# Attention and feed-forward layer on one core: the output projection as three float32r passes, half of it inside the last head pair

## What is computed

```python
xn = _layernorm(x, axis=-1)
qkv = einsum('bsh,oh->bso', xn, w_qkv)                  # 16 heads of width 32
scores = where(causal, einsum('bhqd,bhkd->bhqk', q, k) * scale, min)
attn = einsum('bhqk,bhkd->bhqd', softmax(scores), v)
a = einsum('bsh,oh->bso', attn, w_o)                    # the output projection
gate, up = xn @ Wg.T, xn @ Wu.T                         # 4096 wide, weights are 4-bit codes times scales
out = x + a + (gelu(gate) * up) @ Wd.T
```

## Time and profile before

| | us |
|---|---|
| median of 3 runs | 1840.53 (1839.3 to 1840.86) |
| the profiled execution | 1840.19 |
| its span | 1838.4 |
| TensorE busy in the span | 1796.9 |
| VectorE, GpSimd, ScalarE busy | 1127.0, 721.6, 702.3 |

### The profile page before, as it was taken

The page is one execution under the profiler, slowest core; times in us unless marked ns, Lnnn a source line. Parts: engine busy times, 40 slices in busy tenths (PEclk is TensorE's granted clock), DMA queues, the critical chain, the costliest instruction groups (busy, mean ns, idle before and its releaser), DMA issues.

```text
span 1838.4 us, 28874 instructions
## 1 busy us (share of the span) xinstructions
PE 1796.9 (98%) x10496; PEld 1348.4 (73%) x10496; DVE 1127.0 (61%) x1724; ACT 702.3 (38%) x1151; POOL 721.6 (39%) x720
## 2 busy tenths in 40 slices
PE   7989999999999998999999999999999999999998
PEld 6877666666666654478888888888888888888887
DVE  5416666666666666457665675666566567566654
ACT  3323666666666664023232332232232323323322
POOL 1431778778778774021222222222222222222221
PEclk9999999999999998999999999999999999999999
DMA  8675043143143100521101101100110110110002
GB/s 286 218 215 151 10 102 73 37 102 73 37 102 72 38 17 21 197 69 35 35 0 34 34 0 34 34 26 9 34 34 0 34 34 3 31 34 0 1 1 92
DMA packets 73105, 108.59 MB, mean 59 GB/s; under 512 B 24704, under 2 KB 44784, under 8 KB 69360
## 3 DMA queue, kind: packets, MB, share of 16 engines
q1 hardware_dynamic: 73008, 107.34, 21.2%
HBM read 74.04 MB, written 29.59 MB: 56 GB/s over the span
## 4 chain that ended last, share of the span: by engine, by line
PE 60%; DVE 0%; issue 0%
PE p_up L51 6%; PE p_gate L51 6%; PE p_gate L49 6%; PE p_up L49 6%; PE p_gate L50 6%; PE p_up L50 6%; PE p_out L51 6%; PE p_out L49 6%; PE p_out L50 6%; PE p_out L1358 1%; PE p_gate L1358 1%; PE p_up L1358 1%; DVE acc L1288 0%
## 5 line engine op out<-in xcount | busy, mean ns | idle before, releaser
L1200 POOL TENSOR_SCALAR poly<-poly 128x1024 f32<-128x1024 f32 (+1 forms) x65 | 71.4, 1098 | 841.3 <-ACT poly L1162 841.3
L635 POOL TENSOR_TENSOR e_sum<-e_sb 128x512 f32<-128x512 f32 (+1 forms) x244 | 291.2, 1220 | 99.2 <-PE p_o L923 89.8
L771 DVE TENSOR_REDUCE max_part<-p_s 128x1 f32<-128x512 f32 x384 | 241.2, 683 | 51.5 <-PE p_s L855 50.2
L708 ACT ACTIVATE e_sb<-p_v 128x512 f32<-128x512 f32 (+3 forms) x427 | 216.5, 552 | 129.7 <-PE p_v L883 70.2
L1263 DVE SCALAR_TENSOR_TENSOR inter<-inter,gate 128x1024 f32<-128x1024 f32 (+1 forms) x65 | 78.6, 1209 | 248.4 <-ACT inter L1168 247.6
L855 PE MATMUL p_s<-k_stack,q_stack 96*128 96x512 f32 (+3 forms) x640 | 217.2, 393 | 0.7 <-DVE max_part L771 0.5
L767 DVE CUSTOM_DVE_ANT_0 recip<-p_s,score_mask 128x128 bf16<-128x128 f32 (+3 forms) x256 | 119.7, 486 | 156.0 <-PE p_s L855 153.9
L1161 ACT ACTIVATE gate<-p_gate 128x1024 f32<-128x1024 f32 (+1 forms) x65 | 66.0, 1015 | 354.6 <-PE p_gate L51 354.6
L49 PE MATMUL p_gate<-xn_hi,w_hi 128*128 128x512 f32 x512 | 199.6, 390 | 0.0
L50 PE MATMUL p_gate<-xn_lo,w_hi 128*128 128x512 f32 x512 | 199.2, 389 | 0.0
L51 PE MATMUL p_gate<-xn_hi,w_lo 128*128 128x512 f32 x512 | 199.2, 389 | 0.0
(11 more groups left out here) (146 smaller groups left out, 3090.6 us busy)
## 6 DMA issues: line engine op xcount, KB each, us to landing
q_stack<-qk_scratch SPq DMA_DIRECT2D x48, 256.0 KB, 6.5
k_stack<-qk_scratch SPq DMA_DIRECT2D x48, 256.0 KB, 7.2
qk_scratch<-out_hi SPq DMA_DIRECT2D x32, 256.0 KB, 2.6
qk_scratch<-out_lo SPq DMA_DIRECT2D x32, 256.0 KB, 3.3
scales<-in_gate_up_s SPq DMA_DIRECT2D x128, 64.0 KB, 2.3
xn_lo_scratch<-xn_lo SPq DMA_DIRECT2D x4, 1024.0 KB, 5.2
v_scratch<-o_sb SPq DMA_DIRECT2D x16, 256.0 KB, 2.6
xn_lo<-xn_lo_scratch SPq DMA_DIRECT2D x1, 4096.0 KB, 16.7
```

Of the source, the lines that this page charges most:

```text
L635: nc.gpsimd.tensor_tensor(*operands(k, i), ALU.add).then_inc(pool_summed, 1)
L708: nc.scalar.activation(e_sb[:, x % E_BUFS, 0:w], bank_st(x)[:, 0:w], ACT.Exp, scale=SCALE).then_inc(exp_done, 1)
L771: nc.vector.reduce_max(part, p_s[:, slot[n] % S_BUFS, 0:w], AX.X).then_inc(maxed, 1)
```

## The change

The projection is split like the other products: `w_o` into `wo_hi` and `wo_lo`, attention's output into a high part (copied by ScalarE) and a low part (subtracted by GpSimd), with three float32r matmuls for each product (`project_high`, `project_low`). A tile is one of four channel groups for one block of 512 tokens: 12 matmuls over four banks.

- The eight tiles of tokens 0 to 1023 are done in attention's block, in the four banks of `p_s`: four tiles in groups 75 to 78, between the transposed scores, and four behind group 79. The high and low parts have two slots each in a `k_stack` that is free by then. The weights are split in groups 70 to 74, into the `q_stack` of the even pairs. VectorE adds x for tokens 0 to 511 before the last division.
- The eight tiles of tokens 1024 to 2047 open the next block, with six slots in the second half of the weights' buffers.
- The first chunk of packed weights, and x for tokens 0 to 1023, are loaded in attention's block, into `rsum_rows`, `v_stack0`, `wo_sb` and a `k_stack`. In the next block x and `xn_lo` come in parts.
- At the front the values have six slots (four in `rsum_rows`, two in `o_sb`), the heads of pair 0 are loaded in halves, and units stand behind the tiles 5 to 14, five behind each: 50 instead of 44.

The core of the diff, with empty lines taken out:

```diff
+def project_high(nc, banks, g, wo_hi, wo_lo, a_hi, ots):
+    for ot in ots:
+        o = slice(ot * P, (ot + 1) * P)
+        nc.tensor.matmul(banks[ot], wo_hi[:, g, o], a_hi, start=g == 0, stop=False)
+        nc.tensor.matmul(banks[ot], wo_lo[:, g, o], a_hi, start=False, stop=False)
+def project_low(nc, banks, g, wo_hi, a_lo, ots):
+    for ot in ots:
+        last = nc.tensor.matmul(banks[ot], wo_hi[:, g, ot * P:(ot + 1) * P], a_lo, start=False, stop=g == KT - 1)
+    return last
...
+    V_SLOTS = 6
+    FIRST_COLS = S // 2
...
-    BEHIND_V = {v: 4 if v == 6 else 5 for v in range(6, TT - 1)}
+    BEHIND_V = {v: 5 for v in range(5, TT - 1)}
...
+        q_stack = [[stack_hi, stack_lo], [sb(f"q_stack1{a}", [P, S], F32R) for a in range(2)]]
+        k_stack = [[sb("k_stack00", [P, S], F32R)], [sb(f"k_stack1{a}", [P, S], F32R) for a in range(2)]]
+        xt_at = nc.sbuf_base
+        k_stack[0].append(sb("k_stack01", [P, S], F32R))
+        v_stack = [v_stack0[:, :].rearrange("p (t a d) -> p t a d", t=TT, a=2),
+                   sb("v_stack1", [P, TT, 2, D], F32)[:, :, :, :]]
...
+        LAST = NG - NS // GS
+        WO_GROUP = 5
+        WO_TILES = 2 * KT
...
+        xt_0 = nc.alloc_sbuf_tensor_at("xt_0", [P, KT, W], F32, offset=xt_at)[:, :, :]
...
+        def attn_hi(m):
+            return k_stack[0][0][:, (m % 2) * W:(m % 2 + 1) * W]
+        def attn_lo(m):
+            return k_stack[0][0][:, (2 + m % 2) * W:(3 + m % 2) * W]
...
+        def v_slot(v):
+            slot_v = v % V_SLOTS
+            return rsum_rows[:, slot_v * W:(slot_v + 1) * W] if slot_v < TC else \
+                o_sb[:, slot_v - TC, :, :].rearrange("p b w -> p (b w)")
...
-            load_head(sp, 0, 0)
+            for a in range(2):
+                load_head(sp, 0, a, slice(0, FIRST_COLS), first_loaded[a])
             for v in range(TT):
-                if v == 1:
-                    load_head(sp, 0, 1)
+                if v == 2:
+                    for a in range(2):
+                        load_head(sp, 0, a, slice(FIRST_COLS, S))
                 if v in (9, 11):
                     load_head(sp, 1, v // 11)
                 sp.wait_ge(v_out, v + 1)
                 sp.dma_start(v_scratch[v * P:(v + 1) * P, :, :],
-                             o_sb[:, v % 2, :, :].rearrange("p b (h d) -> p (b h) d", d=D)).then_inc(v_stored[v % 2], 16)
+                             v_slot(v).rearrange("p (h d) -> p h d", d=D)).then_inc(v_stored[v % V_SLOTS], 16)
...
-            sp.wait_ge(wo_loaded, 16)
+            sp.wait_ge(st_ready, (PAIRS - 1) * NS * PIECES)
+            sp.dma_start(xt_0, x_t[:, 0:W].rearrange("(k p) t -> p k t", p=P)).then_inc(xt_first, 16)
+            sp.wait_ge(wo_lo_made, KT)
+            sp.dma_start(wo_sb[:, :, :], x_t[:, W:2 * W].rearrange("(k p) t -> p k t", p=P)).then_inc(xt_loaded, 16)
+            sp.wait_ge(pv_done, (PAIRS - 1) * NS)
+            sp.wait_ge(normalised, (PAIRS - 1) * TC)
+            load_first_chunk(sp)
+            sp.wait_ge(xt_first, 16)
+            sp.wait_ge(xt_loaded, 16)
...
+            def split_attn(m):
+                pool.wait_ge(attn_hi_made, m + 1)
+                nc.gpsimd.tensor_tensor(attn_lo(m), attn_tile(m), attn_hi(m).bitcast(F32),
+                                        ALU.subtract).then_inc(attn_lo_made, 1)
...
+                if k - LAST >= WO_GROUP - 1:
+                    split_attn(k - LAST - WO_GROUP + 1)
+            for m in range(NG - LAST - WO_GROUP + 1, WO_TILES):
+                split_attn(m)
...
-                if v >= 2:
-                    act.wait_ge(v_stored[v % 2], 16 * (v // 2))
-                nc.scalar.activation(o_sb[:, v % 2, :, :].rearrange("p b w -> p (b w)"), bank_st(v), ACT.Copy).then_inc(v_out, 1)
+                if v >= V_SLOTS:
+                    act.wait_ge(v_stored[v % V_SLOTS], 16 * (v // V_SLOTS))
+                nc.scalar.activation(v_slot(v), bank_st(v), ACT.Copy).then_inc(v_out, 1)
...
+            def wo_part(g):
+                act.wait_ge(wo_loaded, 16)
+                act.wait_ge(st_ready, (PAIRS - 1) * NS * PIECES)
+                nc.scalar.activation(wo_hi[:, g, :], wo_sb[:, g, :], ACT.Copy).then_inc(wo_hi_made, 1)
+            def attn_high(m):
+                c, g = divmod(m, KT)
+                act.wait_ge(normalised, TC * (PAIRS - 2) + (c + 1 if g == KT - 1 else 0))
+                if g == KT - 1:
+                    act.wait_ge(divided, 4 * (c + 1))
+                if m >= 2:
+                    act.wait_ge(wo_tiled, m - 1)
+                nc.scalar.activation(attn_hi(m), attn_tile(m), ACT.Copy).then_inc(attn_hi_made, 1)
...
+                if 0 <= k - LAST < KT:
+                    wo_part(k - LAST)
+                if k - LAST >= WO_GROUP - 1:
+                    attn_high(k - LAST - WO_GROUP + 1)
+            for m in range(NG - LAST - WO_GROUP + 1, WO_TILES):
+                attn_high(m)
...
+                if 0 < k - LAST <= KT:
+                    g = k - LAST - 1
+                    dve.wait_ge(wo_hi_made, g + 1)
+                    nc.vector.tensor_tensor(wo_lo[:, g, :], wo_sb[:, g, :], wo_hi[:, g, :].bitcast(F32),
+                                            ALU.subtract).then_inc(wo_lo_made, 1)
+            dve.wait_ge(wo_tiled, KT)
+            dve.wait_ge(xt_first, 16)
+            nc.vector.tensor_tensor(attn_t[:, :].rearrange("p (k t) -> p k t", k=KT)[:, :, 0:W], xt_0, p_s[:, :, :],
+                                    ALU.add).then_inc(wo_added, 1)
...
-                if u < 2:
+                if p == 0 and u < 2:
+                    pe.wait_ge(first_loaded[a], 96)
+                elif u < 2 if p else u in (SECOND, SECOND + 1):
                     pe.wait_ge(qk_loaded[p % PB][a], 96 * (p // PB + 1))
...
+            banks = [p_s[:, ot, :] for ot in range(KT)]
+            def project(m, part):
+                if part == 0 and m == 0:
+                    pe.wait_ge(wo_lo_made, KT)
+                    pe.wait_ge(maxed, NUNIT)
+                    pe.wait_ge(max_rows, 2 * len(turn_index))
+                if part == 0 and m == KT:
+                    pe.wait_ge(wo_added, 1)
+                if part == 0:
+                    pe.wait_ge(attn_hi_made, m + 1)
+                if part < 4:
+                    project_high(nc, banks, m % KT, wo_hi, wo_lo, attn_hi(m), (part,))
+                else:
+                    if part == 4:
+                        pe.wait_ge(attn_lo_made, m + 1)
+                    last = project_low(nc, banks, m % KT, wo_hi, attn_lo(m), (2 * (part - 4), 2 * (part - 4) + 1))
+                    if part == 5:
+                        last.then_inc(wo_tiled, 1)
...
+                tile = k - LAST - WO_GROUP
                 def some_units(part, parts):
                     for n in units[part * len(units) // parts:(part + 1) * len(units) // parts]:
                         scores(n)
+                    if 0 <= tile < NG - LAST - WO_GROUP - 1 and part < 6:
+                        project(tile, part)
...
+            for m in range(NG - LAST - WO_GROUP - 1, WO_TILES):
+                for part in range(6):
+                    project(m, part)
...
+        xt_slots = {1: (wo_sb[:, 0:2, :], wo_sb[:, 2:4, :]), 2: (gate[:, :, :], poly[:, :, :]),
+                    3: (inter[:, :, :], scales[1])}
+        WO_CHUNKS = (2, 3)
+        RING = 6
...
+            load_x(2)
+            load_xn_lo(0)
+            load_x(3)
+            for tc in range(1, TC):
+                load_xn_lo(tc)
+            sp.wait_ge(wo_added, 2 * (TC - 1))
+            load(sp, 1, 1)
...
+            for m in range(len(WO_CHUNKS) * KT):
+                if m >= RING:
+                    act.wait_ge(wo_tiled, m - RING + 1)
+                nc.scalar.activation(ring(w_hi[1], m), attn_tile(m), ACT.Copy).then_inc(attn_hi_made, 1)
...
-            act.wait_ge(wo_added, 2 * TC)
+            act.wait_ge(wo_added, 2 * (TC - 1))
...
+                pool.wait_ge(attn_hi_made, m + 1)
+                nc.gpsimd.tensor_tensor(ring(w_lo[1], m), attn_tile(m), ring(w_hi[1], m).bitcast(F32),
+                                        ALU.subtract).then_inc(attn_lo_made, 1)
...
-            for tc in range(TC):
-                if tc < 3:
-                    unpack(0, 0, tc, 1, first=True)
-                    lo_weights(0, 0, tc)
-                dve.wait_ge(xt_loaded[tc], 32)
-                dve.wait_ge(wo_projected, tc + 1)
+            for m in range(3):
+                tc = m + 1
+                dve.wait_ge(xt_loaded[tc], 16 if tc == 1 else 32)
+                if tc in WO_CHUNKS:
+                    dve.wait_ge(wo_tiled, KT * (WO_CHUNKS.index(tc) + 1))
                 for half in range(2):
-                    nc.vector.tensor_tensor(acc[:, 2 * half:2 * half + 2, tc * W:(tc + 1) * W], xt_slot(tc, half),
+                    nc.vector.tensor_tensor(acc[:, 2 * half:2 * half + 2, tc * W:(tc + 1) * W], xt_slots[tc][half],
```

(83 more changed lines are left out.)

100 lines of the change are left out of this document (52 added, 48 removed).

## The result

The changed kernel takes 1817.78 us (median of 4 runs, 1816.53 to 1818.86) against 1840.64 for the kernel before: a ratio of 0.9874 (95% interval 0.986 to 0.9888), 22.9 us less. The forecast was 1811.0: the direction and the range hold, the size is 6.8 us too good. 1817.8 lies outside the narrower 1807 to 1816 that had a chance of 0.58, and beside the numbers of rival 1 (1817.4) and rival 2 (1817.8). The profiled execution took 1818.86 us, its span 1817.1, so the two profiled ones lie 21.3 us apart, where the sum had 29.2.

The account below looks back on a forecast made before the run. TensorE was taken to bound most of the kernel, with waits and low clock at attention's front and gaps in the last pair. Terms -6.8 + 3.5 + 0.3 - 26.2 = -29.2 took 1840.2 to 1811.0 us; range 1804.5 to 1819.

Parts of the forecast that it names:

- rival 1: Last pair: VectorE's and GpSimd's sums collide, five subtractions each delaying by 1.28 us, 6.4 us added: 1817.4; chance 0.15.
- rival 2: Front of attention: no gain, as TensorE waits behind value 5 for the heads' first halves: 1817.8; chance 0.10.
- Part A: Front of attention: six value slots remove waits and low clock, less the cost of six more units: -6.8 us.
- the 7.5 priced: Front of attention: TensorE's waits of 3.37 and 1.75 us and 2.4 us of low clock go, together 7.5 us.
- Group 0 then has 8 units instead of 12: First attention group: four units fewer give 0.9 us back against the 1.6 us that six more units cost.
- Part B: Last head pair: four tiles' matmuls in groups 75 to 78 cost +3.5 us, and group 79 pays +0.3 us.
- four subtractions on VectorE: Last pair: the low weights' subtractions, placed with ScalarE's copies in groups 70 to 73; no separate price given.
- my 1.4 us: Last pair: what its lowered clock was taken to be worth in the kernel before; denser matmuls should keep it up.
- Rival 4: Whole projection: interruptions hold TensorE at its lower clock for all 192 matmuls, 39.0 us more: 1850.0; chance 0.03.
- Part C: Last row sums to first gate product: 36.0 us instead of 62.2, -26.2 us, including third-weights delay.
- The addition: Behind group 79: the fifth tile waits 0.9 us for VectorE's addition over the four score banks.
- The delay behind the gate product: Next block: late third weights delay ScalarE's gate copies and the first inner product, 0.9 us, bounds 0 and 2.3.

Follow-up runs that it names:

- the front alone: The kernel before with only six value buffers, head stacks loaded in halves and 50 score units behind the value tiles; old projection: 1834.96 us, ratio 0.9966.
- the last two kernels: Changed kernel with 44 units, low weights first, ScalarE's copies first, addition by banks: 1809.98 us; the same with GpSimd's subtraction ahead of its normalisation: 1808.55 us.

## Why the prediction was right or wrong

**Part A, right, in part by luck.** -7.2 for -6.8, and -7.2 again for the front alone, so rival 2 is out, though its number, 1817.8, came true to the digit. The waits gave more than the 7.5 priced, 8.3 (70.05 to 61.78 us with 44 units), and the six units cost 1.1 instead of 0.7; the two errors nearly cancel. What I missed is what six more units do afterwards. "Group 0 then has 8 units instead of 12" counted their saving in one group and stopped; they moved the units of every later group that has any, up to 72. A term of +2.5 was absent.

**Part B, too small.** Groups 70 to 79 cost 5.9 for 3.8; groups 75 to 78 took 33.4 us (690.88 to 724.28) for 30.5, outside my bounds of 29.7 to 32.4. (From 29.7 the lower bound would be +2.8, not the +1.5 that I wrote.) I priced TensorE's added matmuls and ScalarE's gaps, and left out what the new work waits for. Two such waits, 1.36 and 1.23, are shown by their removal (-1.28 and -1.25). Both are places in a queue. The "four subtractions on VectorE" had no price, and I put them in groups 70 to 73; they stand in 71 to 74, each behind sums that wait for TensorE, and the last is done only after group 75 has begun (691.39 + 1.76 us against 690.88). GpSimd's subtraction stood behind its normalisation, and I had looked only at what it delays, not at what delays it.

**The clock.** In the last pair it stayed up, as I counted, but that was worth more than my 1.4 us: the kernel before has two falls there, so at 1.5 to 1.7 us for each the last pair's added work costs some 3 us more than the 5.9, an estimate. Behind group 79 it fell, and I had looked for a fall one pause later: +1.6, the price of eight matmuls at 0.43 instead of 0.227 (1.62). Rival 4's mechanism appeared, for 8 matmuls out of 192. The Trainium skill (TensorE: Matmul & The Clock Gate, "What's actually happening") has an idle TensorE fall and sustained work raise it again; that the fall ended after eight matmuls agrees. It set in behind waits of 0.66, 0.33 and 1.45 us, but with the first four matmuls behind the last wait still 0.23 us apart, and the same waits brought no fall in three other kernels: why it comes or stays out is open. The trace is of the slowest of the four runs; the fastest, 1816.53 us, had a mean granted clock of 1.000 and not 0.999.

**Part C.** The eight tiles (21.90 for 21.8) and the block's start were right. The addition was waited for 1.45 us, not 0.9: VectorE came to it right ahead of the last row sums, as I had it, but TensorE was through with these 0.66 us after they began and not, as before, 1.15. The clock is not the reason: it was 1.00 there in both. Before, the row sums overlap in the records with the products ahead of them, now they start 0.33 us late, behind a wait for VectorE's last sum, with these products done. The delay behind the gate product was 2.7 for 0.9, outside its bounds: I took 5.4 us for each unpacking, and the first took 10.9 beside GpSimd, which pushed the third weight past the slack that I had counted. Without GpSimd's subtractions this delay is 1.0 us (2.7 less 1.7), close to the 0.9 of the sum, so the step that failed here is the price of the first unpacking.

**Rival 1 gave nearly the right number, 1817.4, and mostly for a reason that doesn't hold.** Without GpSimd's subtractions groups 70 to 79 gain 2.4 us, of which about 1.25 is order and not collision, so at most 1.2 is left for the collision; 6.4 was its price. The collision is real in the other place, where I had not put it. The Trainium skill (SBUF, "SBUF: two separate sides") says the port pair is held for a whole instruction and the other engine blocks; three of VectorE's four steps of 0.42 us became 1.40 to 1.51, about one GpSimd subtraction each (eight took 11.68 us), which agrees. The page gives that rule for a VectorE instruction with two SBUF inputs or in a mode that takes both ports; these steps have one input, and no view here shows their mode. Of the 7.9 us that I missed, the 2.5 of the pairs are in no rival, and the 1.6 of the clock only as rival 4, at 39.0.

The parts: 0.2 (start) - 0.4 + 2.5 + 2.1 + 1.7 + 1.8 = 7.9 us.

## What to carry over

Work that is moved into gaps costs little only if its inputs stand early in the queues of the engines that make them: for each new instruction look at what is ahead of it on its own engine, not only at what is behind. A count that shifts a schedule, here six units, acts in every later round; multiply its effect by the rounds before calling it nothing. When a rival's number comes true, test its mechanism before taking it as the cause.

## What the runs showed of the hardware

- Between 660 and 750 us the granted clock fell in six of eleven traces: at 690, 720 and 730 in the kernel before, at 730 in the changed one, at 715 and 725 with the front alone, at 680 and 735 without tiles in the groups, at 680 in the last two kernels; never in the other five. The falls at 725 to 735 of the two kernels with plain float32 products stand behind a pause of over 4 us of TensorE, the others behind waits of 0.2 to 2.4 us. Two traces whose matmul starts agree from 660 us to the fall at 680 differ in it. A fall of the second kind cost 1.5 to 1.7 us where it could be compared, more than several of the edits here, so these are better read from their stages than from their totals.
- A GpSimd subtraction of 128x512 beside VectorE stretched three of VectorE's one-input integer steps from 0.42 to between 1.40 and 1.51 us, and seven steps from 4.26 to 10.87.
- The first value tile started between 114.94 and 116.91 us in the eleven traces, with the same work ahead of it: 2.0 us of scatter, as much as an edit here. TensorE's very first instruction already starts between 9.23 and 10.39 us; where the rest arises is not traced.
